# Norm products of subtiles 1 to 3 as three one-pass terms instead of one full 32-bit product

## What is computed

```python
q = hidden_states @ Wq.T                      # per head
sigma_q = elu(q) + 1.0
a_unnorm = jnp.einsum('bhsd,nhde->nbhse', sigma_q, memories)
norm = jnp.einsum('bhsd,nhd->nbhs', sigma_q, memory_norms)
a = a_unnorm / jnp.clip(norm, EPS, None)[..., None]
a = a * active[:, None, None, None, None]
combined = jnp.einsum('nbhse,hn->bhse', a, softmax(bank_weights, axis=-1))
out = combined.transpose(0, 2, 1, 3).reshape(b, s, HID) @ Wo.T
```

## Time and profile before

| | us |
|---|---|
| median of 3 runs (lowest, highest) | 1440.79 (1440.64, 1441.23) |
| the profiled execution, its own time | 1440.71 |
| its span, first to last instruction | 1438.9 |

### The profile page before, as it was taken

The page is one execution under the profiler, slowest core; times in us unless marked ns, Lnnn a source line. Parts: engine busy times, 40 slices in busy tenths (PEclk is TensorE's granted clock), DMA queues, the critical chain, the costliest instruction groups (busy, mean ns, idle before and its releaser), DMA issues.

```text
span 1438.9 us, 18704 instructions
## 1 busy us (share of the span) xinstructions
PE 1396.5 (97%) x6866; PEld 1140.9 (79%) x6866; DVE 880.3 (61%) x1260; ACT 507.9 (35%) x793; POOL 546.5 (38%) x367
## 2 busy tenths in 40 slices
PE   8999999998989999999999999999999999999997
PEld 4578888887768888888888887878888888888885
DVE  6777777778575636545555657484655555463644
ACT  4456666665622222222222233332222212222221
POOL 1756666666053313131332334472313233232311
PEclk9999999999999999999999999999999999999999
DMA  6302122213420202021110302230201101020102
GB/s 243 118 31 114 62 88 87 88 58 118 176 77 19 95 0 95 0 95 47 48 66 29 124 29 95 88 124 1 95 23 71 66 29 68 27 95 0 66 0 95
DMA packets 23657, 102.42 MB, mean 71 GB/s; under 512 B 2628, under 2 KB 3140, under 8 KB 13900
## 3 DMA queue, kind: packets, MB, share of 16 engines
q1 hardware_dynamic: 23628, 102.05, 19.0%
HBM read 68.47 MB, written 33.57 MB: 71 GB/s over the span
## 4 chain that ended last, share of the span: by engine, by line
PE 81%; DVE 11%; issue 3%; ACT 3%; DMA 1%; POOL 1%; POOLq 0%; ACTq 0%; DVEq 0%; SPq 0%
PE bank L1107 25%; PE bank L1109 25%; PE bank L1108 25%; PE bank L1178 2%; PE bank L1128 2%; DVE banks_r L936 1%; PE bank L1159 1%; PE bank L1116 1%; DVE h_abs L1059 1%; DVE one_each L1047 1%; PE bank L1188 1%; DVE pair_lo L1041 1%; DVE ln_raw L767 1%; DVE first_wins L1042 1%; ACT h_full L508 1%
## 5 line engine op out<-in xcount | busy, mean ns | idle before, releaser
L1022 DVE TENSOR_TENSOR h_act<-bank,silu_g 128x512 f32<-128x512 f32 x128 | 88.1, 690 | 408.4 <-PE bank L1109 387.7
L451 POOL TENSOR_TENSOR hs_lo<-h_abs,hs_hi 128x512 fp32r<-128x512 f32 x128 | 174.9, 1397 | 417.5 <-ACT hs_hi L671 417.5
L403 POOL TENSOR_TENSOR h_lo<-h_raw,h_hi 128x512 fp32r<-128x512 f32 x64 | 125.1, 1983 | 236.4 <-ACT h_hi L654 236.4
L1107 PE MATMUL bank<-h_hi,up_w_hi 128*128 128x512 f32 x512 | 200.8, 392 | 7.2 <-DVE h_act L1022 6.0
L1107 PE MATMUL bank<-h_hi,gate_w_hi 128*128 128x512 f32 x512 | 200.1, 391 | 5.8 <-ACT silu_g L677 3.0
L1107 PE MATMUL bank<-down_w_hi,hs_hi 128*128 128x512 f32 x512 | 199.6, 390 | 2.9 <-POOL hs_lo L451 2.9
L1108 PE MATMUL bank<-h_lo,up_w_hi 128*128 128x512 f32 x512 | 200.2, 391 | 0.0
L1109 PE MATMUL bank<-h_hi,up_w_lo 128*128 128x512 f32 x512 | 200.1, 391 | 0.0
L1109 PE MATMUL bank<-h_hi,gate_w_lo 128*128 128x512 f32 x512 | 199.5, 390 | 0.0
L1108 PE MATMUL bank<-h_lo,gate_w_hi 128*128 128x512 f32 x512 | 199.5, 390 | 0.0
L1109 PE MATMUL bank<-down_w_hi,hs_lo 128*128 128x512 f32 x512 | 199.2, 389 | 0.0
(11 more groups left out here) (133 smaller groups left out, 2398.9 us busy)
## 6 DMA issues: line engine op xcount, KB each, us to landing
h_raw<-h2T_scratch SPq DMA_DIRECT2D x16, 1024.0 KB, 4.8
x_ring<-in_x_dram SPq DMA_DIRECT2D x8, 1024.0 KB, 4.9
x_scratch<-x_ring SPq DMA_DIRECT2D x8, 1024.0 KB, 3.9
h2T_scratch<-h_full SPq DMA_DIRECT2D x8, 1024.0 KB, 3.9
over_x<-x_scratch SPq DMA_DIRECT2D x8, 1024.0 KB, 4.8
acc_scratch<-over_x SPq DMA_DIRECT2D x8, 1024.0 KB, 3.9
over_x<-acc_scratch SPq DMA_DIRECT2D x8, 1024.0 KB, 4.8
out_dram<-over_x SPq DMA_DIRECT2D x8, 1024.0 KB, 3.9
```

The lines of the kernel that those rows point to most:

```text
L403: nc.gpsimd.tensor_tensor(h2_lo[:, k], h2_raw[:, k], h2_hi[:, k].bitcast(F32), ALU.subtract).then_inc(h2_lo_done, 1)
L451: nc.gpsimd.tensor_tensor(hs_lo[:, j], h_abs[:, j], hs_hi[:, j].bitcast(F32), ALU.subtract).then_inc(hs_lo_done, 1)
L1022: nc.vector.tensor_tensor(h_act[:, cc, j], bank[2 * (j % 2) + 1][:], silu_g[:, j % 2], ALU.mult).then_inc(h_done, 1)
L1107: nc.tensor.matmul(out_, stat[0], mov[0], start=start, stop=False)
```

## The change

For subtile 0 of each tile `norms` stays as it was. For subtiles 1, 2 and 3 it calls `mm3` with `sigma_hi`, `sigma_lo` and two new constant tiles, `norm_hi` and `norm_lo`, which DVE makes once in the setup by a rounding copy and a subtraction. To order these after the four copies and after each other, DVE waits on its own semaphore (`link`) twice. `sigma_hi` and `sigma_lo` are there already, for `banks_of`.

```diff
+            norm_hi = sba("norm_hi", [P, K, NB * HG], F32R)
+            norm_lo = sba("norm_lo", [P, K, NB * HG], F32R)
...
                 ins = nc.vector.tensor_copy(norm_cols[rows, :, hh // PAIR, :, hh % PAIR], norm_raw[rows])
-            ins.then_inc(norm_bd_ready, 1)
+            link(ins)
+            norm_flat = norm_bd[:].rearrange("p k n h -> p k (n h)")
+            link(nc.vector.tensor_copy(norm_hi[:], norm_flat))
+            nc.vector.tensor_tensor(norm_lo[:], norm_flat, norm_hi[:].bitcast(F32),
+                                    ALU.subtract).then_inc(norm_bd_ready, 1)
             h1_low(0, 2)
...
             def norms(u, s):
                 for g in range(K):
                     cols = slice(g * NB * HG, (g + 1) * NB * HG)
-                    ins = nc.tensor.matmul(bank[6][:, cols], sigma[:, g, s * P:(s + 1) * P],
-                                           norm_bd[:, g].rearrange("p n h -> p (n h)"), start=True, stop=True)
+                    toks = slice(s * P, (s + 1) * P)
+                    if s == 0:
+                        ins = nc.tensor.matmul(bank[6][:, cols], sigma[:, g, toks],
+                                               norm_bd[:, g].rearrange("p n h -> p (n h)"), start=True, stop=True)
+                    else:
+                        ins = mm3(bank[6][:, cols], (sigma_hi[:, g, toks], sigma_lo[:, g, toks]),
+                                  (norm_hi[:, g], norm_lo[:, g]), True, True)
                 ins.then_inc(norm_done, 1)
```

## The result

Six runs of each kernel: 1446.16 us median (1444.7 to 1448.06) with the change, 1440.85 us (1440.41 to 1441.23) before. The ratio is 1.0039, 95% interval 1.0026 to 1.0052: slower by 0.39%, 5.3 us. The forecast was 1447.7 us, range 1444.4 to 1450.9. The profiled execution took 1446.49 us, with a span of 1444.7 against 1438.9.

What follows compares the result with a forecast made beforehand. PE, busy for 97% of the span, was taken to bound the kernel. 15 of 24 groups at 0.43 us (6.5 us) plus 0.5 us setup, 7.0 us on 1440.71, gave 1447.7 us, range 1444.4 to 1450.9.

Steps and rivals of the forecast that it cites:

- The price of a group: Norm group on PE: twelve loads at 0.110 us take 1.32 us in place of 0.89, 0.43 us more.
- Rival 1: Norm groups: one-pass loads are short, 0.065 us a pair, so a group takes 0.11 us less; 1439.6 us, chance 0.07.
- Which groups are on the path: Middle tiles: subtiles 1 and 3 add 0.43 us each, subtile 2 nothing; 0.86 us a tile, 5.2 us for six.
- Rival 2: Middle tiles: all three groups of a tile count, 3.0 us more, 1450.7 us; chance 0.12.
- rival 3: Middle tiles: DVE's waits hide subtile 1's delay, only subtile 3's groups count; 3.9 us added, 1444.7 us, chance 0.10.
- Subtile 3: PE's stream has no wait around it: Middle tiles, norms of subtile 3 on PE: nothing hides the group, so it adds its whole 0.43 us.
- the 0.72 us at the transposes: Middle tiles: PE's wait for ACT at the transposes takes up 0.27 us of subtile 2's delay, shrinking to about 0.45.
- Setup: DVE's copy and subtraction for the new constants delay PE's first products; 0.5 us added, bounds 0.2 and 0.6.
- PE works without a break from there to the norms: Setup: from its first products to the norms PE has no wait, so the 0.5 us delay passes on whole.
- Tile 0 and the last tile: Tile 0: groups of subtiles 2 and 3 count, 0.9 us; last tile: only subtile 1's group, 0.4 us.
- rival 4: Clock fall in the last tile goes or moves: some 2.3 us either way, 1445.4 or 1450.0 us; chance 0.12.

Runs made afterwards that it cites:

- subtile 1 alone: Three one-pass terms in the norms of subtile 1 only, subtiles 0, 2 and 3 in full 32 bits; ratio 1.0017 to the kernel before.
- two terms: The changed kernel without the term with `norm_lo`, so eight one-pass loads a group; ratio 0.9996 to the kernel before.
- subtile 2 alone: Three one-pass terms in the norms of subtile 2 only, the other subtiles in full 32 bits; ratio 1.0003 to the kernel before.
- subtile 3 alone: Three one-pass terms in the norms of subtile 3 only, the other subtiles in full 32 bits; ratio 1.0012 to the kernel before.
- the repeat: The changed kernel run once more, unaltered; median 1446.03 us, ratio 1.0039 to the kernel before.
- the constants alone: The kernel before plus `norm_hi` and `norm_lo` made in the setup but not used, all groups in full 32 bits; ratio 1.0004.
- filled kernel before: The kernel before with unread products of ones, seven at each of three PE waits in tile 0 and the last tile; ratio 0.9991.
- filled changed kernel: The changed kernel with the same unread products of ones in PE's waits; 1445.39 us, ratio 1.0022 to the kernel before.
- D: Not a run: time from subtile 0's norms in tile 1 to those in the last tile; 237.56 us before, 242.30 with the change.

## Why the prediction was right, and where it was not

1. **The price of a group** was right: 0.43 us more predicted, 1.34 against 0.89 us measured behind `wo_product`, that is 0.45 (0.44 in the kernel with subtile 1 alone). It comes from the number of weight loads: 4 loads a group took 0.43 us, 8 took 0.88, 12 took 1.34, and neither the type (two terms) nor the columns (16 or 64) changed that. Rival 1, short one-pass loads, is refuted: loads of 128 x 128 in the one-pass type start 0.11 us apart. The reading of the fast weight load rule by which this type would profit falls with it. The Trainium skill, "TensorE: Matmul & The Clock Gate", section "LDWEIGHTS", gives 107 ns for such a load, and the trace agrees.
2. **Which groups are on the path** was right: subtile 1 by way of DVE, subtile 3 on PE, subtile 2 not. Rival 2 (all three) and rival 3 (only one) are refuted by the kernels with one subtile each. The size a tile was 0.79 in place of 0.86 us, since PE had waited a tenth for DVE behind subtile 3 before, and that wait took up as much. The step "Subtile 3: PE's stream has no wait around it" was the one that was off. The place that hides subtile 2 was named wrongly in part: the waits for POOL (0.31 us, not 0.16) and for `x_ring`, not the 0.72 us at the transposes, which I had said would shrink to 0.45.
3. **Setup**: the step "PE works without a break from there to the norms", from which I took 0.5 us, failed. It was 0.0, outside my bounds of 0.2 and 0.6. Of the two lines that ran to the first norms I followed PE's, where the delay was 0.23 us and not 0.5; PE's products of the modulation rows waited for DVE's, which had the delay in reserve.
4. **Tile 0 and the last tile**: in tile 0 the two groups counted as said; from its first norms to those of tile 1 it is 48.16 us after (40.80 to 88.96) and 47.27 before (41.67 to 88.94), 0.89 more against 0.86. The clock is the same in both (0.76 from 48 to 62 us), and also with subtile 2 alone (47.75) and subtile 3 alone (47.74). A comparison across clocks would mislead: the repeat of the changed kernel, at 0.88, takes 46.98 us, and the kernel with the constants alone, at 0.88 too, 46.22. In the last tile rival 4 came in beside my forecast.

The first product with the up weights, timeline of the kernel before and then of the changed one:

```profile
362.74 0.50 PE L1107 MATMUL bank<-h_hi,up_w_hi 128*128 128x512 f32 x1
```

```profile
366.97 0.50 PE L1113 MATMUL bank<-h_hi,up_w_hi 128*128 128x512 f32 x1 [0.61 <-DVE up_w_lo L918]
```

From the last tile's first norms it is 36.24 us before and 35.71 after: 0.53 less, where 0.44 more was due. The windows say why, 343 to 355 us of the changed kernel:

```profile
343.00:355.00 12.00, 8.37 (x59) 7.22 (x58) 11.83 (x20) 5.76 (x11) 6.29 (x6) 0.86 0.47 176
```

The granted clock is 0.86 there in place of 0.72: PE is at 1.2 GHz for a shorter time, and for bank products in the place of the twelve products from 349.25. Where the clock is 1.00 in both, in the two filled kernels, the same stretch takes 35.34 us (filled kernel before) and 35.75 (filled changed kernel): 0.41 more, the one group that I had forecast. So the path was right there, and the clock hid it. Rival 4 had put its size at 2.3 us; it was about 1 (0.53 + 0.44).

Between these two profiles the second phase takes back more than that. It is the same code in both and takes 1076.2 us before (from 362.74 to the end) and 1077.7 after. In the first 10 us behind PE's long wait the clock is 0.85 before and 0.74 after:

```profile
409.00:419.00 10.00, 9.92 (x37) 8.12 (x38) 1.41 (x3) 3.22 (x7) 3.04 (x3) 0.85 0.01 2
```

```profile
413.30:423.30 10.00, 10.00 (x34) 8.07 (x35) 1.38 (x2) 3.13 (x7) 2.95 (x3) 0.74 0.00 0
```

But 1.5 us is well inside the 1076.1 to 1079.9 us that this code takes from profile to profile, so it is no effect of the change that is shown. The span is cut at unchanged instructions, so its pieces must add up and prove nothing by it; they say where the 5.8 us between the two profiles lie: 0.9 us earlier at the first norms (the modulation rows' transposes came at 16.75 in place of 17.63 us, ahead of anything the change touches), +0.89 in tile 0, +4.74 in the middle tiles, -0.53 in the last and +1.5 in the second phase.

By the path alone the change costs 0.89 + 4.74 + 0.44 = 6.1 us, where I had 6.5 + 0.5 = 7.0. The whole time says 5.3 us by the medians and 5.6 by the ratio, and in the repeat 4.8 and 5.6. That the rest is the clock is consistent with the two profiles of the changed kernel, which both have the shorter fall in the last tile; how often it comes so in the other runs was not measured and stays open. The whole time alone would not have decided for me: 1446.16 us lies nearer to rival 4's 1445.4 than to my 1447.7, and my range held rivals 2, 3 and 4 as well. D and the kernels with one subtile decide.

## What to carry to other kernels

A product with few moving columns costs its weight loads, so splitting it into three terms makes it dearer by half against a full 32-bit product, which the trace records with two loads. With many columns it is the other way round: in the setup the four full 32-bit products of 512 columns from 38.15 to 41.67 us of the kernel before take 0.88 us each (their stationary operand has 4 columns only), and three one-pass terms of 512 columns, 0.23 us apart, take 0.68. Before counting an added cost once for each place, ask in each place which engine is behind: here a third of the groups in the middle tiles were free, and a cost in the setup was free because both lines had a reserve. When the whole time tells only a few tenths of a per cent, find two unchanged instructions around the changed stretch, with no fall of the clock between them, and measure from one to the other; that told 0.1 us here (237.46 to 237.56 in the five profiles whose middle tiles should be equal).

## What the runs showed that I had not expected

Work taken off PE gave less than the same work added cost: four loads fewer in a group saved 0.26 us a tile, four more cost 0.79, since PE and DVE are level at two places of a tile (DVE's scaling of subtile 1, and `wo_product` behind subtile 3). And the clock falls in other places from kernel to kernel even where the code is the same; why was not tested. The changed kernel, the same in its second phase, had the clock at 0.83 from 885 to 905 us in both of its profiles, the kernel before at 0.91 and the filled changed kernel at 1.00.
